# First convolution as fp32 products on four quadrants, in place of split products on the whole array

## What is computed

```python
scores = einsum('bhwke,bhwe->bhwk', neighbourhood(x) @ K_P, x @ Q_P) * mask
attn = einsum('bhwk,bhwke->bhwe', softmax(scores), neighbourhood(x) @ V_P)
t_in = x + attn
t = relu(conv(t_in, ff1) + b1)      # conv1
u = relu(conv(t, ff2) + b2)         # conv2
w = relu(conv(u, ff3) + b3)         # conv3
return t_in + w
```

## Time and profile before

| | |
|---|---|
| median of 3 runs | 2454.2 us |
| the profiled execution's own time | 2453.68 us |
| its span, first to last instruction | 2451.8 us |
| TensorE (PE) busy | 2249.4 us |
| VectorE (DVE) busy | 2035.9 us |
| ScalarE (ACT) busy | 1234.8 us |
| mean granted TensorE clock | 0.979 of 2.4 GHz |

### The profile page before, as it was taken

One profiled execution on the slowest core, in us unless ns is written; L12 is line 12 of the kernel. 1 busy time (PEld: TensorE's weight loads), 2 busy tenths in 40 slices (PEclk: granted clock), 3 DMA queues, 4 the chain that ended last, 5 costly groups with the idle time before them and its releaser, 6 DMA issues.

```text
span 2451.8 us, 60325 instructions
## 1 busy us (share of the span) xinstructions
PE 2249.4 (92%) x22404; PEld 1386.0 (57%) x22404; DVE 2035.9 (83%) x2909; ACT 1234.8 (50%) x3238; POOL 15.3 (1%) x23
## 2 busy tenths in 40 slices
PE   4899999999899999999879999999988999999997
PEld 3655655565556555655555556556555555565554
DVE  4888888887688888888768888888867888888886
ACT  2555555553455555555355555555535555555543
POOL 2000000000000000000000000000000000000000
PEclk7999999999899999999989999999998999999999
DMA  5545544553355445545454555455434554554453
GB/s 126 158 128 142 164 136 142 147 155 120 118 147 163 139 136 153 154 128 141 127 150 140 139 153 152 129 140 166 141 113 136 153 151 128 142 164 137 141 144 120
DMA packets 296942, 346.98 MB, mean 142 GB/s; under 512 B 86244, under 2 KB 220196, under 8 KB 290212
## 3 DMA queue, kind: packets, MB, share of 16 engines
q1 hardware_dynamic: 296812, 345.26, 49.5%
HBM read 152.77 MB, written 33.82 MB: 76 GB/s over the span
## 4 chain that ended last, share of the span: by engine, by line
PE 72%; DVE 14%; issue 8%; ACT 4%; DVEq 1%; DMA 1%; SPq 1%; ACTq 0%
PE conv_banks L459 27%; PE conv_banks L473 14%; PE conv_banks L436 10%; PE mix_bank L413 5%; PE conv_banks L440 5%; DVE work L790 4%; DVE dtl L757 3%; ACT dth L640 3%; PE score_banks L398 3%; PE mix_bank L424 3%; DVE tf L727 2%; DVE work L741 2%; PE score_banks L387 2%; PE proj_bank L420 1%; PE score_banks L395 1%
## 5 line engine op out<-in xcount | busy, mean ns | idle before, releaser
L459 PE MATMUL conv_banks<-dodd,w3f 128*64 128x512 f32 (+1 forms) x1656 | 500.1, 579 | 13.5 <-DVE dodd L741 8.4
L459 PE MATMUL conv_banks<-deven,w3f 128*64 128x512 f32 (+1 forms) x1656 | 490.1, 566 | 0.0
L573 ACT ACTIVATE prob<-score_banks,negmax 128x100 f32<-128x100 f32 x1040 | 341.5, 361 | 170.8 <-DVE negmax L707 170.8
L473 PE MATMUL conv_banks<-duh,w2h 64*128 64x512 f32 (+2 forms) x1632 | 358.6, 419 | 9.5 <-DVE work L790 5.5
L790 DVE TENSOR_TENSOR work<-conv_banks,work 128x1024 f32<-128x1024 f32 (+3 forms) x273 | 310.7, 1159 | 55.5 <-PE conv_banks L459 42.6
L473 PE MATMUL conv_banks<-duh,w2l 64*128 64x512 f32 (+2 forms) x1632 | 325.4, 379 | 0.0
L640 ACT CAST dth<-work 128x1024 fp32r<-128x1024 f32 x130 | 136.4, 1050 | 293.4 <-DVE work L741 292.7
L473 PE MATMUL conv_banks<-dul,w2h 64*128 64x512 f32 (+2 forms) x1632 | 281.3, 378 | 0.0
L459 PEld LDWEIGHTS conv_banks<-dodd,w3f 128*64 128x64 f32 x1656 | 138.7, 137 | 230.3 <-issue 202.8
L473 PEld LDWEIGHTS conv_banks<-duh,w2h 64*128 64x128 f32 x1632 | 166.8, 184 | 142.8 <-issue 103.7
L707 DVE TENSOR_REDUCE negmax<-score_banks 128x4 f32<-128x400 f32 x260 | 142.0, 568 | 117.7 <-PE score_banks L387 104.7
(11 more groups left out here) (93 smaller groups left out, 3727.8 us busy)
## 6 DMA issues: line engine op xcount, KB each, us to landing
xk<-x_keys SPq DMA_DIRECT2D x66, 800.0 KB
xc<-x_bands SPq DMA_DIRECT2D x67, 650.0 KB, 5.7
dodd<-dodd SPq DMA_DIRECT2D x68, 512.0 KB, 3.0
xr<-x_bands SPq DMA_DIRECT2D x264, 128.0 KB, 4.9
kept<-tf SPq DMA_DIRECT2D x129, 256.0 KB, 5.1
out<-work SPq DMA_DIRECT2D x60, 512.0 KB, 2.7
dth<-dth SPq DMA_DIRECT2D x68, 256.0 KB, 2.3
dtl<-dtl SPq DMA_DIRECT2D x68, 256.0 KB, 2.5
```

The costliest lines, as they stand in the source:

```text
L459: return nc.tensor.matmul(bank[rows, lo * 128:hi * 128], w3f[:, m, s, odd * C:odd * C + C], source[:, lo + s // 2:hi + s // 2, m], start=s ...
L473: return nc.tensor.matmul(conv_banks[:, bank_of(which, j), lo * 128:hi * 128], w[rows, STREAMS[j], 2 * (which == EVEN) + s], d[rows, lo + ...
L573: last = nc.scalar.activation(prob[:, g % 2, a], score_banks[:, g % 2, a * KEYS:(a + 1) * KEYS], ACT.Exp, bias=negmax[:, g % 2, a:a + 1], ...
```

## The change

The first convolution no longer has high and low parts: its input dt and its weights are plain fp32, and `t_high` and `t_low` are gone. Each product takes one image's 64 columns of up to 4 row pairs (256 columns), one row half as input and one output half, so one of four quadrants (64 x 64) of the array. The two row halves may not write the same output half at once, so the work has two phases for the middle and two for the outer streams (`begin1`, `end1`), with a two-column matmul between; scores of the first half stand between the last two. For image 1 odd and even rows change sides, in `xr` and in the V product's outputs, so that both images fill all quadrants; a second set of weights (`w1f[1]`) has its halves exchanged, and `kept` exchanges the rows back with three transfers in place of one. The two products of a pair of streams lie in one bank, image 0 and image 1 in two. The order of conv3's tiles is 0, 2, 1, 3, ODD takes banks 0 and 1 and EVEN 2 and 3, `go_on2(0)` goes ahead of `mix(0)`, and ACT's and DVE's orders are changed to match.

```diff
-        w1h = sb("w1h", [128, 4, 2, 128], F32R)
-        w1l = sb("w1l", [128, 4, 2, 128], F32R)
+        w1f = [sb(f"w1f{i}", [128, 4, 2, 128], F32) for i in range(2)]
...
 @block.sync
             def load_xr(b):
                 for i in range(2):
-                    for odd in range(2):
-                        sp.dma_start(xr[odd * C:odd * C + C, :, i],
+                    for odd, rows in ((i, LOWER), (1 - i, UPPER)):
+                        sp.dma_start(xr[rows, :, i],
...
+            def keep(to, at, par, lo):
+                for i, rows, image in ((0, FULL, FULL), (1, LOWER, UPPER), (1, UPPER, LOWER)):
+                    sp.dma_start(kept[rows, to, at:at + 2, i],
+                                 tf[image, par, lo:lo + 2, i, 1:1 + W]).then_inc(carried, 16)
...
-            for dst, src in zip(raws, (w1, w2, w3)):
+            sp.dma_start(raws[0], w1).then_inc(w_in, 16)
+            for rows, other in ((LOWER, UPPER), (UPPER, LOWER)):
+                sp.dma_start(raws[1][rows], w1[other]).then_inc(w_in, 16)
+            for dst, src in zip(raws[2:], (w2, w3)):
...
-                sp.wait_ge(tile_done, filled(G, CONV1, 3))
-                for t in (dth, dtl):
-                    sp.dma_start(t[:, 0:1].bitcast(F32), t[:, RP:RP + 1].bitcast(F32)).then_inc(t_kept, 16)
+                sp.wait_ge(conv1_done, G * 8 + 8)
+                sp.dma_start(dt[:, 0:1], dt[:, RP:RP + 1]).then_inc(t_kept, 16)
 @block.tensor
+            def tap1(k, i, m, n, rows, o, s, start, stop):
+                lo, hi = pairs1(k)
+                if k == 0 and s == 0:
+                    lo = 1
+                bank = conv_banks[:, i if m in (1, 2) else 2 + i]
+                return nc.tensor.matmul(bank[(LOWER, UPPER)[o], n * 256 + lo * 64:n * 256 + hi * 64],
+                                        w1f[i][rows, m, s, o * C:o * C + C], dt[rows, lo + s:hi + s, m, i],
+                                        start=start, stop=stop)
+            def begin1(k, m, n, last):
+                taps = (0,) if k == BANDS else (1, 0)
+                for s in taps:
+                    for i, rows, o in ((0, LOWER, 0), (0, UPPER, 1), (1, UPPER, 0), (1, LOWER, 1)):
+                        mm = tap1(k, i, m, n, rows, o, s, n == 0 and s == taps[0],
+                                  n == 1 and o == 1 and k == BANDS)
+                        if last and s == taps[-1]:
+                            mm.then_inc(conv1_half, 1)
+            def begin1_middle(G, k, b):
+                pe.wait_ge(dt_done, b * 2 - 1)
+                pe.wait_ge(t_kept, G * 16 + 16)
+                pe.wait_ge(dve_read, outer_read(G, ODD, 1))
+                nc.tensor.matmul(conv_banks[:, 0, 0:2], eye16_sb[:], window_sb[:, 0:2], start=True, stop=True)
+                begin1(k, 2, 0, False)
+                begin1(k, 1, 1, True)
+            def begin1_outer(G, k, b, n):
+                if n == 0:
+                    pe.wait_ge(dt_done, b * 2)
+                    pe.wait_ge(dve_read, outer_read(G, EVEN, 1))
+                    nc.tensor.matmul(conv_banks[:, 2, 0:2], eye16_sb[:], window_sb[:, 0:2], start=True, stop=True)
+                begin1(k, (0, 3)[n], n, n == 1)
+            def end1(G, k, outer):
+                pe.wait_ge(conv1_half, G * 8 + (8 if outer else 4))
+                nc.tensor.matmul(conv_banks[LOWER, 2 * outer, 0:2], eye16_sb[:, LOWER], zeros16[:], start=False, stop=False)
+                for n in range(2):
+                    m = ((2, 1), (0, 3))[outer][n]
+                    for i, rows, o in ((1, LOWER, 0), (1, UPPER, 1), (0, UPPER, 0), (0, LOWER, 1)):
+                        if o == 1 and k == BANDS:
+                            continue
+                        mm = tap1(k, i, m, n, rows, o, o, False, n == 1)
+                        if n == 1:
+                            mm.then_inc(conv1_done, 2 if k == BANDS else 1)
 # TensorE's step
                     r_product(b, par)
+                begin1_middle(G, k, b)
+                begin1_outer(G, k, b, 0)
+                end1(G, k, False)
+                begin1_outer(G, k, b, 1)
+                if att:
                     scores(b, par, 0)
-                pe.wait_ge(t_kept, G * 32 + 32)
-                for j in ORDER1:
-                    conv1_tile(G, k, b, j)
+                end1(G, k, True)
                 conv3_tile(G, k, 0)
-                conv3_tile(G, k, 1)
+                conv3_tile(G, k, 2)
                 if att:
                     turn(b, 0)
-                conv3_tile(G, k, 2)
+                conv3_tile(G, k, 1)
...
                 begin2(G, k, 0)
+                go_on2(G, k, 0)
                 if att:
                     mix(b, 0)
                 begin2(G, k, 1)
-                go_on2(G, k, 0)
                 go_on2(G, k, 1)
```

More of the change, by code:

```diff
@@ L151, in build @@
         w_in = sem("w_in")
-        w_stage = sem("w_stage")
+        w1_stage = [sem(f"w1{i}_stage") for i in range(2)]
         w2_stage = sem("w2_stage")
@@ L421, in v_product @@
                 moving = y[:].rearrange("c a (r s) -> c a r s", s=PATCH)
-                for odd, to in enumerate((LOWER, UPPER)):
-                    for bank, image in ((mix_bank, UPPER), (proj_bank, LOWER)):
+                for odd in range(2):
+                    for i, bank, image in ((1, mix_bank, UPPER), (0, proj_bank, LOWER)):
+                        to = UPPER if odd != i else LOWER
                         mm = nc.tensor.matmul(bank[to].rearrange("c (a r s) -> c a r s", r=RP, s=PATCH),
@@ L564, in _ @@
             schedule(pe, step)
-            for j in range(4):
+            for j in ORDER3:
                 conv3_tile(ALL_STEPS, 0, j)
@@ L660, in _ @@
             keep_y(0, 1)
-            for part in range(2):
-                t_high(None, 0, part)
             act.wait_ge(pool_zeroed, 1)
             def step(G, k, b, q, par, att):
+                if k:
+                    relu_conv2(G, k - 1, ODD, 1)
                 if att:
@@ L693, in step @@
                     keep_y(b, 1)
-                    for part in range(2):
-                        t_high(G, b, part)
                 if k == BANDS:
@@ new lines, in outer1 @@
+            def outer1(G, k):
+                dve.wait_ge(conv1_done, G * 8 + 8)
+                dve.wait_ge(dve_read, middle_read(G, CONV1))
+                if k < BANDS:
+                    m03 = conv_banks[:, 2:4].rearrange("c i (s w) -> c s i w", w=WT)
+                    both = sums1.rearrange("c n s i w -> c (n s) i w")
+                    nc.vector.tensor_tensor(both, m03, both, ALU.add).then_inc(dve_read, 1)
+                else:
+                    lo, hi = pairs1(k)
+                    for n in range(2):
+                        m = conv_banks[:, 2:4, n * 256 + lo * 64:n * 256 + hi * 64]
+                        last = nc.vector.tensor_tensor(sums1[:, n, lo:hi], m.rearrange("c i (s w) -> c s i w", w=WT),
+                                                       sums1[:, n, lo:hi], ALU.add)
+                    last.then_inc(dve_read, 1)
@@ new lines, in outer3 @@
+            def outer3(G, k):
+                lo, hi = pairs3(k)
+                dve.wait_ge(tile_done, filled(G, CONV3, 3))
+                dve.wait_ge(dve_read, middle_read(G, CONV3))
+                for n in range(2):
+                    m = conv_banks[:, bank_of(CONV3, 2 + n)].rearrange("c (s i w) -> c s i w", i=2, w=WT)[:, lo:hi]
+                    o = sums[CONV3][:, lo:hi, :, n::2]
+                    last = nc.vector.tensor_tensor(o, m, o, ALU.add)
+                last.then_inc(dve_read, 1)
@@ L823, in _ @@
             for part in range(2):
-                t_inputs(0, 0, part)
-            for part in range(2):
-                t_low(0, part)
+                t_inputs(None, 0, 0, part)
             def step(G, k, b, q, par, att):
@@ L831, in step @@
                     outer(G, k - 1, EVEN, 1)
+                    inputs(G, k - 1, ODD, 0, 1)
+                    inputs(G, k - 1, EVEN, 0, 1)
+                middle1(G, k)
                 if att:
@@ L868, in step @@
                     for part in range(2):
-                        t_inputs(b, par, part)
-                    for part in range(2):
-                        t_low(b, part)
+                        t_inputs(G, b, par, part)
                 if k == BANDS:
```

156 lines of the change are left out of this document (65 added, 91 removed).

## The result

The changed kernel takes 2530.57 us (median of 4 runs, 2522.15 to 2535.5) against 2453.95 us before on the same chip: 1.0308 of it, interval 1.0295 to 1.0322, so **77 us slower** where 52 us faster was forecast. Its profiled execution has a span of 2528.9 us.

The account below looks back on a forecast made before the run. TensorE, busy 92% of the span, was taken as the bound. Interior steps -26, bands without attention -16, between pairs -9, start +1 and end -2 sum to -52 us: forecast 2402 us, range 2372 to 2450.

Parts of the forecast that it names:

- the one that costs the added products: First convolution on TensorE: 96 instructions in 24 waves take 5.2 us, with fences 0.6 us more work a step.
- the slower rival: First convolution: fences and waves at their upper bounds, 8.6 us in place of 7.4, near 2470 us; chance 0.13.
- The waves: First convolution on TensorE: four quadrants overlap, 0.2175 us a wave (between 0.213 and 0.24), 24 waves 5.2 us.
- The rival that row halves take turns: First convolution: row halves writing one bank alternate, 48 waves for 24, 5.2 us more a step, near 2755 us; chance 0.02.
- The fences: First convolution: four two-column products a step, 0.23 us each with restart, 0.9 us together; bounds 0.11 and 0.4 each.
- The idle time: Turn between bands: TensorE idles 0.3 to 0.4 us in place of 1.49, a gain of 1.1 us a step.
- The covers: Inside a step: ACT's and DVE's results still arrive in time, the thinnest spare 0.6 us before the transposes.
- SP: Transfers of kept's rows: six issues a step for two, 2.6 us more on SP, costed at nothing.
- The band without attention: Last full band, four times: shorter chain and perhaps no clock drop, 4 us earlier each, -16 us.
- Between the pairs: Three turns to a new pair: conv1 no longer waits for ACT, gain 1 to 5 us, taken as 3 each, -9 us.
- the +0.6 of band 16: Band 16: conv1 is tiny, so conv3 waits for DVE's middle transforms, about +0.6 us.
- Start and end: First weights and kernel end: +1 us at the start (-2 to +5), -2 us at the end without low parts.

Follow-up runs that it names:

- run 1: Changed kernel with TensorE's twelve middle bands of a pair written out instead of looped: 2394.89 us, 0.976 of the kernel before.
- run 4: Kernel before with only kept's rows in three transfers each, six issues a band on SP for two: 2452.86 us, ratio 1.0.
- run 7: Changed kernel with four bands in TensorE's loop body and three turns, in place of two bands and six turns: 2446.05 us, 0.997 of the kernel before.
- run 8: Changed kernel with TensorE's middle bands written out and two unused DVE operations put back where t's low parts stood: 2584.61 us.
- run 2: Kernel before with the same twelve middle bands written out on TensorE, as a control: 2452.38 us, ratio 0.9995.

## Why the prediction was wrong

**The step that failed** is the one that costs the added products. It counts them ("there are 96 instructions" on TensorE) and prices them by their pace alone: "TensorE's arithmetic costs as much as before". The instructions as code, 147 more a band and so 294 in the loop body, had no term. They took the body over a limit that the kernel before stayed under, and each of 20 jumps back then cost 6.8 us: +136 us, more than twice the whole forecast gain. None of the rivals was this one; the slower rival named fences and waves, and the range ended at 2450.

The page of before could have raised the question. Its part 3 has 80 packets of instructions for a program that executes 44808 loads and products on TensorE alone; that is fewer than one packet for 500 of them. By the block of 256 instructions that the Trainium skill gives in the section named above, 80 packets hold 20480; the rest can only have run from what was already there. And its list of waits has TensorE at the head of each new pair:

```profile
PE proj_bank L362 <- issue: 10.5, 3, 3.8
```

The prediction passes over that row. It is the same wait, with an instruction packet in each of the three, at the jump from pair to pair, whose body is a whole pair.

**The other steps**, checked on run 1, where the jumps are away (2394.9 against the forecast of 2402, inside the 2385 to 2425 given for it):

- *The waves*: 0.2175 us taken by the scores' row, 0.2175 measured. The V products' 0.24 was no bound that mattered. The rival that row halves take turns is refuted: a wave of four records took 0.2175 us, where the prediction has 0.213 for the stream of one record alone, with both row halves writing into each bank, each to its own partitions, as in the scores.
- *The fences*: 0.23 taken, about 0.27 measured; none cost 0.4. The section is 7.46 us for 7.3 to 7.4.
- *The idle time*: 0.3 to 0.4 forecast, 0.18 left. So a band is 34.95 where 35.1 was forecast, -0.63 for -0.5, and 52 of them -33 us for -26.
- *The covers*: the transposes, the thinnest, had 0.4 us to spare for the 0.6 counted (DVE's last scaling ends at 1129.84, the fence of the transposes stands at 1130.27). No new wait arose in the middle bands. In band 1 it does exist, 1.44 us, and stands against the shorter turn there: bands 0 and 1 are 0.4 us longer a pair than before.
- *SP*: nothing, as run 4 shows.
- *The band without attention*: 28.9 us from conv1 to conv1 where 31.9 to 33.0 stood, -3.7 for -4; conv1's wait there is 1.42 us in place of 3.92.
- *Between the pairs*: the step before a new pair is 34.1 to 35 us in run 1 for 38.2 to 39.8 before, -4.5, where -3 and the +0.6 of band 16 had been counted. The -3 was a middle value of 1 to 5, so that part of the nearness of the total is luck.
- *Start and end*: conv1 starts at 57.6 us for 55.9, +1.7 for +1; the end is 1.3 shorter for 2. The first of these is not resolved: the profiled runs of the changed kernel, whose code up to there is the same, start conv1 anywhere from 53.7 to 57.8 us.
- *Slips in the sums*: the terms given for TensorE's added work come to about 0 to 1.8 us, not 0.2 to 1.9; 5.8 us behind 6.2 end at 12.0, not 12.2; and the interior gain gone gives 2428 to 2454 us, not 2426 to 2450. None of them moves the forecast.

These terms (-33, -15, -13, +2 for bands 0 and 1, +1.7, -1.3) sum to -59 us, and run 1's span is 59.5 shorter than that of before.

What stays open: whether the change could be made to fit, with 54 to 102 instructions less in the body, was not tried, nor where exactly between 1621 and 1669 the limit lies, nor whether it moves with the body's place in the code, nor what sets the length of a wait at a jump (3.9 to 5.7 us), in which the packet itself takes only 0.9 to 1.5 us.

## What to carry to other kernels

Count the instructions of a loop body before adding to it, and look at the instruction queue in the profile: a kernel whose packets stop inside a loop runs from loaded code, and a wait of 4 to 6 us with no releaser at the head of a turn was the sign here that it no longer does. More and smaller products at the same pace are not free then; where the code grows past the limit, writing the loop out on that one engine gave back everything, since fetching code in sequence cost no time that shows. And cost a change twice, as work and as code: what it takes off the chain was forecast here to 0.13 us a band, and was worth nothing until the loop was gone.

## What the runs showed that I had not expected

- The limit of TensorE's loop body in this kernel, between 1621 and 1669 instructions, and that it is a cliff: 2465.7 us below, 2613.9 above.
- Every wait at such a jump has an instruction packet beginning in it (23 of 23 in the kernel after).
- A jump to code that isn't loaded, in the kernel after: 3.9 to 5.7 us of idle time, and with the half clock behind it 6.8 us on average (6.4 in run 7).
- The clock fell after idle stretches of 4.59 us and, at 19 of 52 turns in run 8, of 2.46 us, and the same 32 instructions took 3.62 and 3.33 us in place of 1.89. A wait's price is then more than its length: 2.28 us put back on DVE cost 190 us over 64 bands, 3.0 each.
- More than twice as many instruction packets (80 to 191, run 2) changed nothing.
